# A third register load, earlier picks and looser scatter waits in the expert stage of an attention and mixture-of-experts kernel

## The reference

```
x = x + tanh(g0) * (attention(norm(x), context) + feed_forward(norm(x)))
n = norm(x)
weights, experts = top 2 of softmax(n @ gate_w.T), weights scaled to sum 1
y[token] = sum over its 2 experts of weight * (silu(n @ up_w[e] + up_b[e]) @ down_w[e] + down_b[e])
x = x + tanh(g1) * (y + silu(n @ sh_up_w + sh_up_b) @ sh_down_w + sh_down_b)
```

## Time and profile before

| | us |
|---|---|
| median of 3 runs (lowest, highest) | 538.68 (537.32, 539.99) |
| profiled execution, its own time | 537.07 |
| its span, first to last instruction | 535.3 |
| PE busy | 494.9 |
| DVE busy | 406.2 |
| ACT busy | 327.2 |
| POOL busy | 291.4 |

### The profile page before, as it was taken

The page is one execution under the profiler, slowest core; times in us unless marked ns, Lnnn a source line. Parts: engine busy times, 40 slices in busy tenths (PEclk is TensorE's granted clock), DMA queues, the critical chain, the costliest instruction groups (busy, mean ns, idle before and its releaser), DMA issues.

```text
span 535.3 us, 13844 instructions
## 1 busy us (share of the span) xinstructions
PE 494.9 (92%) x4026; PEld 480.3 (90%) x4026; DVE 406.2 (76%) x1251; ACT 327.2 (61%) x1092; POOL 291.4 (54%) x334
## 2 busy tenths in 40 slices
PE   7779999999999999999999999999999979999940
PEld 7769999999999999999999999999987869999930
DVE  7687778688887878878788878687777887888830
ACT  3667566756675767566567565756667526767730
POOL 3588636444543755364355436444686334677773
PEclk9999999999999999999999999999999999999995
DMA  5660300121003010200301030023598955778753
GB/s 173 197 223 12 99 2 32 31 81 60 21 20 118 31 30 25 103 32 20 118 21 32 8 120 29 10 79 100 182 335 321 414 194 120 128 136 143 120 65 39
DMA packets 40212, 53.85 MB, mean 101 GB/s; under 512 B 4597, under 2 KB 34218, under 8 KB 39146
## 3 DMA queue, kind: packets, MB, share of 16 engines
q1 hardware_dynamic: 31856, 41.48, 23.8%
q0 software_dynamic: 8000, 11.86, 11.5%
q10 hardware_dynamic: 314, 0.01, 0.1%
HBM read 28.15 MB, written 25.21 MB: 100 GB/s over the span
## 4 chain that ended last, share of the span: by engine, by line
PE 62%; DVE 13%; issue 7%; DMA 6%; ACT 5%; POOLq 3%; POOL 2%; SPq 0%; DVEq 0%; ACTq 0%
PE bank L1548 12%; PE bank L1550 11%; PE bank L1549 11%; PE bank L1629 5%; PE bank L1641 4%; PE bank L1734 4%; DMA out_x<-norm_probs,th 4%; PE bank L1724 4%; POOLq L733 3%; PE bank L1645 3%; PE bank L1632 2%; PE bank L1739 2%; PE bank L1563 2%; DVE norm_probs L1016 2%; ACT norm_probs L822 2%
## 5 line engine op out<-in xcount | busy, mean ns | idle before, releaser
L627 POOL TENSOR_TENSOR norm_probs<-norm_probs,rden 128x512 f32<-128x512 f32 x64 | 66.6, 1041 | 101.2 <-DVE rden L1196 100.7
L1548 PE MATMUL bank<-acts,weights 128*128 128x256 f32 x384 | 109.3, 285 | 4.7 <-POOL weights L598 4.7
L1549 PE MATMUL bank<-acts,weights 128*128 128x256 f32 x384 | 108.0, 281 | 0.0
L1550 PE MATMUL bank<-acts,weights 128*128 128x256 f32 x384 | 107.8, 281 | 0.0
L822 ACT ACTIVATE norm_probs<-bank,nmax 128x128 f32<-128x128 f32 x256 | 90.6, 368 | 24.0 <-DVE nmax L1152 23.9
L632 POOL TENSOR_TENSOR acts<-uf,acts 128x256 fp32r<-128x256 f32 x64 | 47.5, 743 | 68.7 <-ACT acts L810 68.7
L1548 PEld LDWEIGHTS bank<-acts,weights 128*128 128x128 f32 x384 | 72.6, 189 | 5.7 <-issue 4.4
L746 POOL DMA_INDIRECT out_x<-norm_probs,th x39 | 60.7, 1557 | 28.0 <-DMA out_x<-norm_probs,th 13.2
L1550 PEld LDWEIGHTS bank<-acts,weights 128*128 128x128 f32 x384 | 72.5, 189 | 0.0
L1549 PEld LDWEIGHTS bank<-acts,weights 128*128 128x128 f32 x384 | 72.3, 188 | 0.0
L810 ACT ACTIVATE acts<-uf 128x256 fp32r<-128x256 f32 x64 | 26.8, 419 | 61.1 <-DVE uf L1221 61.0
(11 more groups left out here) (252 smaller groups left out, 1545.3 us busy)
## 6 DMA issues: line engine op xcount, KB each, us to landing
parked<-stage SPq DMA_DIRECT2D x12, 512.0 KB, 3.5
weights<-parked SPq DMA_DIRECT2D x6, 1024.0 KB, 9.8
slot_rows<-tf SPq DMA_DIRECT2D x8, 680.0 KB, 6.5
spare<-slot_rows SPq DMA_DIRECT2D x39, 136.0 KB
ct<-in_ctx SPq DMA_DIRECT2D x8, 256.0 KB, 2.7
xs<-in_x SPq DMA_DIRECT2D x8, 256.0 KB, 4.8
stage<-in_L_ffn_up_w SPq DMA_DIRECT2D x8, 256.0 KB, 2.8
stage<-in_L_ffn_down_w SPq DMA_DIRECT2D x8, 256.0 KB, 3.1
```

What stands on the lines that cost most here:

```text
L627: pool.tensor_tensor(pr[:, s % 2], pr[:, s % 2], rden[:, s % 2, :].unsqueeze(2).broadcast_to((P, 4, P)), ALU.mult).then_inc(probs_ready, 1)
L1548: pe.matmul(ps, wts[1], mov[0], start=first, stop=False, skip_group_check=True)
L1549: pe.matmul(ps, wts[0], mov[0], start=False, stop=False, skip_group_check=True)
L1550: return pe.matmul(ps, wts[0], mov[1], start=False, stop=last, skip_group_check=True)
```

## The change

1. The scatter of tile t waits always for the one four back, and for those three, two and one back only where a flag stands. That takes a third column of flags, so a third register load and a third computed threshold per tile on POOL. The turn table gets three more rows of margins and flags and needs a third snapshot of the counts, `hist[2]`, taken in the last attention group (seven groups counted).
2. VectorE picks the token numbers and weights of tiles 0 and 1 in pipeline steps -2 and -1, each as soon as its gather has landed, instead of both in step 0; the pick of tile 2 moves from step 1 to step 0. SP's gathers of tiles 4 and 5 wait also until TensorE has transposed tiles 0 and 1.
3. The low part of the last shared hidden step is made on VectorE before `window_table` and no longer on POOL. `shared_down(3)` comes before TensorE's wait for the window table and its register load. VectorE's own load of the window word comes after `add_shared(2)`.
4. One block in four of the padding rows takes its token numbers from another source.

```diff
-EARLY_GROUPS, LATE_GROUPS = 3, 5
+EARLY_GROUPS, LATE_GROUPS, LAST_GROUPS = 3, 5, 7
...
-        routing = sb("routing", [P, 180])
-        place_at = iter(range(0, 180, 2))
+        routing = sb("routing", [P, 188])
+        place_at = iter(range(0, 188, 2))
...
         weight = route(4).rearrange("p (t c) -> p t c", t=2)
-        hist_t = route(2 * NE).rearrange("p (k e) -> p k e", k=2)
-        hist = [hist_t[:, k, :] for k in range(2)]
+        hist_t = route(3 * NE).rearrange("p (k e) -> p k e", k=3)
+        hist = [hist_t[:, k, :] for k in range(3)]
         weight8 = routing[:, 0:4 * NE].rearrange("p (t c e) -> p t c e", t=2, c=2)
...
         window_tiles = consts[:, 276:276 + WIN_TILES]
-        turns = consts[:, 284:286].bitcast(I32)
-        turn_f = consts[:, 286:288]
+        turns = consts[:, 460:463].bitcast(I32)
+        turn_f = consts[:, 464:467]
         tile_sum, window_f = consts[:, 288:289], consts[:, 289:290]
...
         upto = consts[:, 306:306 + NE * NE].rearrange("p (e f) -> p e f", e=NE)
-        floor = consts[:, 370:386].rearrange("p (k e) -> p k e", k=2)
-        margin = consts[:, 386:410].rearrange("p (k e) -> p k e", k=3)
-        opens = consts[:, 410:426].rearrange("p (k e) -> p k e", k=2)
-        due = consts[:, 426:450].rearrange("p (k e) -> p k e", k=3)
+        slow_table = slow_stage[:, 0:7 * 16].rearrange("p (k e) -> p k e", k=14)
+        margin, due = slow_table[:, 0:7], slow_table[:, 7:14]
+        floor, opens = [slow_stage[:, 128 + 24 * i:152 + 24 * i].rearrange("p (k e) -> p k e", k=3) for i in range(2)]
+        two_before = consts[:, 284:285]
         tile_past = consts[:, 450:458]
...
         shares = consts[:, 486:486 + WIN_TILES]
-        late_early = consts[:, 494:494 + 2 * NE].rearrange("p (k e) -> p k e", k=2)
-        late, early = [late_early[:, k, :] for k in range(2)]
+        missing = consts[:, 386:386 + 3 * NE].rearrange("p (k e) -> p k e", k=3)
         meta = th[:, 0:2 * TILES].rearrange("p (t n) -> p t n", n=2)
...
         h_ready = sem("h_ready")
-        last_h_ready = sem("last_h_ready")
         dn_filled = sem("dn_filled")
...
             for k in range(NPAD):
-                sp.dma_start(pads[:, k, D:ROW], pad_pairs[k % 3].rearrange("p e k -> p (e k)")).then_inc(pads_stored, 16)
+                src = pad_row[:, D:ROW] if k % 4 == 3 else pad_pairs[k % 4].rearrange("p e k -> p (e k)")
+                sp.dma_start(pads[:, k, D:ROW], src).then_inc(pads_stored, 16)
...
                     sp.wait_ge(meta_ready, t - 3)
+                    if t < 6:
+                        sp.wait_ge(gT_filled, t - 3)
                 load_tile(t)
...
                         pool.iota(tile_before, [[0, 1]], base=-1, channel_multiplier=1, allow_small_or_imprecise_dtypes=True)
+                        pool.iota(two_before, [[0, 1]], base=-2, channel_multiplier=1, allow_small_or_imprecise_dtypes=True)
                         pool.iota(window_tiles, [[1, WIN_TILES]], base=0, channel_multiplier=WINDOW,
...
-            for m in range(KT):
-                step = TPS - 1
-                pool.wait_ge(hh_done, step * KT + m + 1)
-                pool.tensor_tensor(hh[:, step % 2, 1, m, :], hf[:, step % 2, m, :], hh[:, step % 2, 0, m, :].bitcast(F32),
-                                   ALU.subtract).then_inc(last_h_ready, 1)
             for j in range(1, TPS):
...
                 if t >= 1:
-                    due_1, due_2 = [pool.value_load(turns[t:t + 1, i:i + 1], min_val=0, max_val=16) for i in range(2)]
+                    due_1, due_2, due_3 = [pool.value_load(turns[t:t + 1, i:i + 1], min_val=0, max_val=16) for i in range(3)]
+                if t >= 4:
+                    pool.wait_ge(y_added[t % 4], 16 * (t // 4) + 16)
                 if t >= 3:
-                    pool.wait_ge(y_added[(t - 3) % 4], 16 * ((t - 3) // 4) + 32)
+                    pool.wait_ge(y_added[(t - 3) % 4], due_3 + (16 * ((t - 3) // 4) + 16))
                 if t >= 2:
...
                     slot_sums(g - 1)
+                    counts_so_far(2)
                     slot_numbers(g - 1)
...
                     dve.memset(shares[:, k:k + 1], float(1 << (SHIFT * k)))
-                dve.tensor_scalar(late, hist[0], -1.0, float(P), ALU.mult, ALU.add)
-                dve.tensor_scalar(early, hist[1], -1.0, 2.0 * P, ALU.mult, ALU.add).then_inc(shares_done, 1)
+                for k in range(2):
+                    done = dve.tensor_scalar(missing[:, k, :], hist[k], -1.0, (k + 1.0) * P, ALU.mult, ALU.add)
+                done.then_inc(shares_done, 1)
                 dve.wait_ge(shares_done, 1)
...
+                dve.wait_ge(ring_ready, NPOS)
+                dve.tensor_scalar(missing[:, 2, :], hist[2], -1.0, 3.0 * P, ALU.mult, ALU.add)
                 link(dve.tensor_scalar(far, ntiles, -float(P), float(P), ALU.mult, ALU.add))
-                link(dve.tensor_tensor(floor, hist_t, far.unsqueeze(1).broadcast_to((P, 2, NE)), ALU.add))
-                dve.tensor_tensor(margin[:, 0:3:2, 0:NE - 1], floor[:, :, 0:NE - 1], late_early[:, :, 1:], ALU.max)
-                dve.scalar_tensor_tensor(margin[:, 1, 0:NE - 1], floor[:, 0, 0:NE - 1], float(P), late[:, 1:], ALU.add, ALU.max)
-                for k, at in enumerate((this_tile, tile_before)):
+                link(dve.tensor_tensor(floor, hist_t, far.unsqueeze(1).broadcast_to((P, 3, NE)), ALU.add))
+
+                dve.tensor_tensor(margin[:, 0:3, 0:NE - 1], floor[:, :, 0:NE - 1], missing[:, :, 1:], ALU.max)
+                dve.scalar_tensor_tensor(margin[:, 3:5, 0:NE - 1], floor[:, 0:2, 0:NE - 1], float(P), missing[:, 0:2, 1:],
+                                         ALU.add, ALU.max)
+                dve.scalar_tensor_tensor(margin[:, 6, 0:NE - 1], floor[:, 0, 0:NE - 1], 2.0 * P, missing[:, 0, 1:],
+                                         ALU.add, ALU.max)
+                for k, at in enumerate((this_tile, tile_before, two_before)):
                     done = dve.tensor_scalar(opens[:, k, 0:NE - 1], ends[:, 0:NE - 1], at, 16.0, ALU.is_equal, ALU.mult)
...
-                dve.scalar_tensor_tensor(due[:, 0:2, 0:NE - 1], margin[:, 0:2, 0:NE - 1], 0.0,
-                                         opens[:, 0:1, 0:NE - 1].broadcast_to((P, 2, NE - 1)), ALU.is_gt, ALU.mult)
-                link(dve.scalar_tensor_tensor(due[:, 2, 0:NE - 1], margin[:, 2, 0:NE - 1], 0.0, opens[:, 1, 0:NE - 1],
-                                              ALU.is_gt, ALU.mult))
+                for rows, at in ((slice(0, 3), slice(0, 3)), (slice(3, 5), slice(0, 2)), (slice(6, 7), slice(0, 1))):
+                    done = dve.scalar_tensor_tensor(due[:, rows, 0:NE - 1], margin[:, rows, 0:NE - 1], 0.0,
+                                                    opens[:, at, 0:NE - 1], ALU.is_gt, ALU.mult)
+                link(done)
                 dve.tensor_reduce(turn_f[:, 0:1], due[:, 0, 0:NE - 1], AX.X, ALU.max)
-                link(dve.tensor_reduce(turn_f[:, 1:2], due[:, 1:3, 0:NE - 1], AX.XY, ALU.max))
+                dve.tensor_reduce(turn_f[:, 1:2], due[:, 1:4:2, 0:NE - 1], AX.XY, ALU.max)
+                link(dve.tensor_reduce(turn_f[:, 2:3], due[:, 2:7:2, 0:NE - 1], AX.XY, ALU.max))
                 dve.tensor_copy(turns, turn_f).then_inc(turns_done, 1)
...
             add_shared(1)
+            hidden_lo(TPS - 1)
             window_table()
+            add_shared(2)
             dve.wait_ge(tables_done, 2)
             experts_of = dve.value_load(window[0:1, 0:1])
-            add_shared(2)
             add_shared(3, (0,))
...
+                if t in (-2, -1):
+                    dve.wait_ge(gathered[t + 2], 16)
+                    pick_meta(t + 2, t + 2)
                 if t > 2 and k == 0:
...
                     add_shared(3, (1,))
-                if t == 0:
-                    pick_meta(0, 0)
-                    pick_meta(1, 1)
                 if t == 1:
-                    pick_meta(2, 2)
                     turn_table()
-                if t >= 1 and runs(t + 2):
+                if t >= 0 and runs(t + 2):
                     pick_meta(t + 2, k + 4)
...
-                if j < TPS - 1:
-                    pe.wait_ge(h_ready, KT * j + KT)
-                else:
-                    pe.wait_ge(last_h_ready, KT)
+                pe.wait_ge(h_ready, KT * j + KT)
                 for t in tiles:
...
             shared_down(2)
+            shared_down(3)
             pe.wait_ge(tables_done, 2)
             experts_of = pe.value_load(window[0:1, 0:1])
-            shared_down(3)
...
                 nonlocal experts_of
...
```

## The result

The changed kernel takes 555.7 us (median of 4 runs, 554.28 to 556.23) against 538.0 us for the kernel before in the same rounds (537.16 to 539.99): a ratio of 1.0306, 95% interval 1.0255 to 1.0356. The profiled execution took 554.28 us, with a span of 552.6.

What follows compares the result with a forecast made beforehand. POOL's sequencer list was taken to bound the tile stage; 23.8 + 2.5 - 0.4 - 2.5 - 0.5 = +22.9 us on 537.07 gave 560.0, and 1.6 more for the runs' median 561.6 us, range 552 to 568.

Steps and rivals of the forecast that it cites:

- What bounds the stage: Tile stage: POOL's sequencer list, not a landing, sets the scatters' pace in nearly every cycle, 2.07 us each.
- The third load: POOL, line 733, tiles 1 to 38: an unhidden register load with check, 0.625 us each, +23.8 us.
- the rival of slow third loads: POOL's load line: every third load is a slow one, +29.1 us in all, 567.8 us; chance 5%.
- The threshold addition: POOL, tiles 3 to 38: due_3 needs an addition of its own, 0.07 us each, +2.5 us.
- The wait three back and the swallowed stalls: POOL's scatters: the loosened wait saves 0.4 us, and the slower cycle covers two flagged stalls, saving 2.5 us.
- The start: Ahead of the scatters: earlier picks bring the first scatter 0.5 us sooner, between -1.9 and +1.0.
- VectorE's account: VectorE before the first gathered tile's split: 1.9 us more work, less 0.40 idle, so the split about 1.4 us late.
- The rest: Third snapshot in the last attention group, added IOTA, padding source and larger tables: zero.
- What would show it: Tile stage: 114 loads, scatters 2.6 to 2.75 us apart, no cycle under 2.4, PE some 70% busy after 480.
- this sign of being wrong: Tile stage: the forecast would be wrong if TensorE's granted clock fell there.
- the 582 of that rival: Tile stage: TensorE takes over as bound, half the tiles at 1.2 GHz, about 582 us; chance 2%.

Runs made afterwards that it cites:

- e9: Changed kernel with its three register loads, each value bounded by a mask (& 16) instead of the range check: 541.66 us, ratio 1.0048 to the kernel before.
- e2: Changed kernel with a fourth register load per tile whose value nothing uses: 573.62 us, ratio 1.0638 to the kernel before.
- e1: Changed kernel with two register loads per tile and the old constant wait three back: 535.14 us, ratio 0.9911 to the kernel before.
- e7: Changed kernel with only the low part of the last shared hidden step back on POOL: 556.25 us, ratio 1.0312 to the kernel before.
- e8: e4 with a second register load of the word per tile that nothing uses: 550.58 us, ratio 1.0216 to the kernel before.
- e4: Changed kernel with a tile's three flags packed in one word, loaded once, same waits: 531.22 us, ratio 0.9871 to the kernel before.
- e5: e4 with the constant wait three back and only two flags taken from the word: 533.52 us, ratio 0.9901 to the kernel before.
- e10: e4 repeated in the same rounds as e11: 530.8 us, ratio 0.9842 to the kernel before.
- e11: e5 repeated in the same rounds as e10: 532.55 us, ratio 0.9873 to the kernel before.

## Why the prediction was right, and where its sizes were off

**What bounds the stage: right.** POOL's sequencer sets the pace by its list. One load fewer (with the old wait) or one more moves the scatters by 18.2 and 19.1 us, and one load in place of three by 22.5 to 23.8, with the front of the change in place.

**The third load: right in kind, too dear by 0.07 us a tile.** The prediction took the mean of the four loads shown, 0.365, and added the check: 0.625. The third load costs a fast load and its check, 0.555 us, its lower bound, and 21.1 us over 38 tiles instead of 23.8. None of the third loads took over 0.30 us, so the rival of slow third loads fell. A slow load is not a share of all loads. In the kernel before the first and second loads took 0.322 and 0.388 us in the mean, 0.355 together; in the kernel after the three took 0.377, 0.291 and 0.290. It even brought a little less: the excess over 0.29 was 0.13 us a cycle before and is 0.09 after, 38 x 0.04 = 1.6 us.

Where a slow load lies can be read in the rows, if its start is counted from the end of the last scatter's own row on POOL. Two scatters, in the kernel before and after, and the slow load behind the second of them:

```profile
481.47 1.55 POOL L746 DMA_INDIRECT out_x<-norm_probs,th  x1 [0.54 <-issue]
```

```profile
485.79 1.55 POOL L745 DMA_INDIRECT out_x<-norm_probs,th  x1 [1.11 <-ACT norm_probs L954]
```

```profile
488.03 0.46 POOLq L730
```

The first ends at 483.02, and of the loads of the earlier trace rows the one at 483.14 (+0.12) is fast and the one at 483.69 (+0.67) is slow and ends at 484.22 (+1.20). The second ends at 487.34; the load at 488.03 (+0.69) is slow and ends at 488.49 (+1.15). So it is over all 13 traces, if what takes over 0.35 us is called slow. Of the 157 loads that begin 0.38 to 0.74 us after that end, all are slow; of the 72 at 0.74 to 0.83, 35 are; of the other 844, 5 are. Of the 197 slow ones 175 end 1.05 to 1.23 us after it. A cycle passes this stretch once, and the list decides which load is in it: mostly the second in the kernel before (20 of 25), the first in the kernel after, in nearly every cycle one in e9. In e2 no load begins between 0.38 and 1.13 us after that end, and hardly one is slow. What happens in the stretch the profile does not show, and no run moved a load alone to test it.

**The threshold addition: right.** Lines 734, 736 and 738 stand 0.07 to 0.08 us apart. With the load, the lists differ by 0.62 us, 23.6 in 38 tiles.

**The wait three back and the swallowed stalls: right, and a little large.** Both stalls are gone. Of +23.6 for the lists and -1.6 for the slow loads, 20.0 were measured, so 2.0 us are left for this term, where 2.9 were taken. That is a remainder, not a measurement of its own. The same remainder between e1 and the kernel after is 3.5 us (23.6 for the lists, less 1.9 for slow loads, less the 18.2 measured).

**The start: the step that failed most.** It was to be 0.5 us sooner, since VectorE would come 1.4 us late with the hidden split; it was 2.65 sooner. The step that failed is VectorE's account: its split of the first gathered tile was not late at all, 435.67 against 435.94 in the earlier trace rows, and in the eight undelayed traces it came 7.66 to 7.69 us after the last send, against 8.72 before. Four rows of VectorE in the kernel after: the hidden split (its two halves), a part of the window table, a pick ahead of the split, and the split; and SyncE's gather of the fifth tile, predicted for 437.5.

```profile
429.49 1.29 DVE L1389 TENSOR_TENSOR q_t<-norm_probs,q_t 128x512 fp32r<-128x512 f32 x2
430.70 0.21 DVE L1425 TENSOR_TENSOR ct<-tf,routing 128x56 f32<-128x56 f32 x1
...
431.19 0.17 DVE L1428 TENSOR_TENSOR ct<-ct,tf 128x8 f32<-128x8 f32 x1
...
435.60 0.17 DVE L1513 COPY th<-spare 128x2 f32 x1 [0.25 <-DVE xs L1445]
435.67 0.42 DVE L1529 TENSOR_TENSOR kz_l<-bank,kz_h 128x256 fp32r<-128x256 f32 x1
```

```profile
435.93 0.33 SPq L553 DMA_DIRECT2D spare<-slot_rows  x1
```

The 1.29 us were there as counted. What was missed is what they gave back. In the kernel before the same two table operations took five times as long, on VectorE, while POOL's 2.52 us of the earlier trace rows ran:

```profile
428.70 1.12 DVE L1424 TENSOR_TENSOR ct<-tf,routing 128x56 f32<-128x56 f32 x1
...
430.11 0.90 DVE L1427 TENSOR_TENSOR ct<-ct,tf 128x8 f32<-128x8 f32 x1
```

And in e7, with the split back on POOL (2.52 us from 430.13) and nothing else:

```profile
430.37 1.11 DVE L1431 TENSOR_TENSOR ct<-tf,routing 128x56 f32<-128x56 f32 x1
...
431.76 0.90 DVE L1434 TENSOR_TENSOR ct<-ct,tf 128x8 f32<-128x8 f32 x1
```

(1.12 + 0.90) - (0.21 + 0.17) = 1.64 us came back to VectorE, more than the 1.29 that it took on. A second wait went too. In the kernel before VectorE then stood for a product of TensorE, which itself stood 1.56 us for the window table; none of the eight undelayed traces has this wait:

```profile
432.10 2.46 DVE L1398 SCALAR_TENSOR_TENSOR xs<-bank,gates,xs 128x512 f32<-128x512 f32 x3 [0.71 <-DVE tf L1429]
```

1.29 - 1.64 - 0.71 = -1.06 us, and 7.67 - 8.72 = -1.05 was measured. The kernel after had 0.8 us of it taken away by its late product.

The sign of the 1.64 us was in the trace of before: 1.12 us for 56 columns beside 0.21 for the reduction of the same 56 columns. The two are not slowed by a factor: each ends just after the POOL operation beside it. POOL's 2.52 us are two operations; the first ends at 429.76 and VectorE's at 429.83, the second at 430.99 and VectorE's other at 431.01. The Trainium skill (SBUF — State Buffer, Who interferes with whom) says that a VectorE instruction with two SBUF inputs contends with a GpSimd instruction that reads SBUF, and that the lock on the ports they share is exclusive. The trace agrees for the two with two inputs: 1.12 and 0.90 us beside POOL's work and 0.21 and 0.17 without; the reduction between them, with one input, kept its 0.21.

**The rest: right.** The third snapshot, the IOTA and the padding show nowhere; the end behind the last scatter is 9.70 us against 9.74.

**What would show it.** 114 loads, as said. The scatters are 2.60 us apart in the mean, from 2.36 to 3.15, where 2.6 to 2.75 and no cycle under 2.4 were named (one of 38 is, at 2.36, just after the start, where ScalarE's tile ended the wait of the scatter ahead); the third load at +0.555, the low end of what was named. ScalarE waits for landings 13 times, as said. TensorE's fall to some 70% was named for 480 and came at 510: while the ring of eight fills, it runs at its own pace. The clock did fall, at 520, but nothing hung on TensorE by then: this sign of being wrong came, and the 582 of that rival did not.

## What to carry to other kernels

A flag that a queue has to load is not free because it only loosens a wait: a register load with its check and its addition cost 0.62 us in every one of 38 cycles, for waits that were worth some 2 to 3.5 us in all by the remainders. Before loosening waits, read whether the queue that waits has any idle time; if its own list fills the cycle, shorten the list (here flags packed in one word, which turned +3.1% into -1.3 to -1.6%) and expect the next floor close below. Where a small operation has an odd duration beside its neighbours', look at what the engine next to it ran at the time, because moving that work can give back more than it costs. And before a small difference of two profiled executions is put down to an edit, look whether another kernel with the same code in that place agrees: here one execution was 0.8 us late by itself.

## What the runs showed of the hardware

- A register load on POOL's sequencer: 0.282 to 0.30 us in most cases, up to 0.714, and 0.555 us from one to the next with its range check; 0.32 without the check. Unused results cost the same (e2, e8).
- A register load that began 0.38 to 0.74 us after the end of a scatter's row on POOL took 0.36 to 0.71 us (157 of 157 in 13 traces), and most slow loads ended 1.05 to 1.23 us after that row; 5 of 844 loads before or after this stretch (outside 0.38 to 0.83) were slow. The cause was not found.
- The indirect scatter of 128 x 256 holds POOL for 1.55 us, and the next starts no sooner than 0.30 us after it, also where the list is shorter (e4, e5, e10, e11).
- VectorE operations with two SBUF inputs of 56 and 8 columns stretched from 0.21 and 0.17 to 1.12 and 0.90 us beside POOL operations of 128 x 512 (before, e7): each ended 0.02 to 0.07 us after the POOL operation beside it.
